# Per-event step tables and twelve collecting parts of three tiles in a four-layer graph kernel

## The reference

```python
x = _layernorm(x + attention(x, adj))            # 4 heads of 16: leaky scores, masked softmax over neighbours, relu
x = _layernorm(x + (adj + I) @ x / rowsum(adj + I))
x = _layernorm(x + adj @ (x @ W) + bias)
x = _layernorm(x + where(adj @ x > 0.5, 1, 0))
```

## Time and profile before

| what | us |
|---|---|
| median of 3 runs | 1550.73 |
| lowest, highest | 1539.59, 1557.88 |
| profiled execution, own time | 1557.14 |
| its span, first to last instruction | 1555.3 |

### The profile page before, as it was taken

The page is one execution under the profiler, slowest core; times in us unless marked ns, Lnnn a source line. Parts: engine busy times, 40 slices in busy tenths (PEclk is TensorE's granted clock), DMA queues, the critical chain, the costliest instruction groups (busy, mean ns, idle before and its releaser), DMA issues.

```text
span 1555.3 us, 20985 instructions
## 1 busy us (share of the span) xinstructions
PE 1374.7 (88%) x7296; PEld 692.2 (45%) x7296; DVE 1243.9 (80%) x1498; ACT 1223.9 (79%) x1404; POOL 1053.2 (68%) x562
## 2 busy tenths in 40 slices
PE   4798898998989999998999989899999989799766
PEld 2343444554444444444444544444444444345323
DVE  2779899778888778778897888888788888977764
ACT  1599898887878878788888878888788888878641
POOL 3177777767778766787677786777667876866412
PEclk9889899899999999999999999999999999989968
DMA  6734453243433433333343344335333433100000
GB/s 96 113 34 78 42 98 43 54 47 53 74 44 71 44 68 57 58 57 38 85 57 63 39 57 80 44 67 48 64 54 65 57 37 84 38 15 15 26 10 11
DMA packets 140879, 84.95 MB, mean 55 GB/s; under 512 B 100372, under 2 KB 130522, under 8 KB 140762
## 3 DMA queue, kind: packets, MB, share of 16 engines
q1 hardware_dynamic: 125542, 64.67, 19.9%
q0 software_dynamic: 14160, 18.51, 15.1%
q10 hardware_dynamic: 1072, 0.43, 0.1%
HBM read 103.33 MB, written 21.38 MB: 80 GB/s over the span
## 4 chain that ended last, share of the span: by engine, by line
PE 50%; POOL 12%; ACT 12%; issue 12%; DVE 11%; DMA 2%; SPq 1%; ACTq 0%; POOLq 0%; DVEq 0%
PE M L603 10%; PE Z L569 10%; PE M L658 9%; PE Z L576 8%; POOL LS L502 8%; ACT LS L750 6%; PE Z L587 4%; ACT LS L758 4%; PE Z L672 3%; PE Z L612 3%; DVE LS L912 3%; DVE RP L898 2%; POOL RSTD L507 2%; DMA adj_cast<-in_adj_dram 1%; PE Z L726 1%
## 5 line engine op out<-in xcount | busy, mean ns | idle before, releaser
L502 POOL TENSOR_TENSOR LS<-LS,MB 125x1000 f32<-125x1000 f32 x372 | 867.1, 2349 | 354.3 <-DVE LS L912 290.4
L750 ACT ACTIVATE LS<-Z 126x1000 f32<-126x1000 f32 x576 | 575.5, 1000 | 168.5 <-PE Z L576 167.3
L898 DVE TENSOR_TENSOR RP<-LS,RP 125x1000 f32<-125x1000 f32 x480 | 575.5, 1199 | 86.0 <-ACT LS L750 65.0
L758 ACT ACTIVATE LS<-LS 125x1000 f32<-125x1000 f32 x576 | 596.4, 1036 | 45.8 <-POOL LS L502 26.8
L569 PE MATMUL Z<-AT,BI 126*126 126x500 fp8e4 x1152 | 381.2, 414 | 78.0 <-ACT LS L750 50.4
L576 PE MATMUL Z<-FS,FO 128*125 128x500 f16 x1152 | 361.5, 396 | 0.0
L603 PE MATMUL M<-LS,V 126*18 126x500 f32 x2304 | 323.9, 637 | 3.9 <-ACT LS L758 3.8
L569 PEld LDWEIGHTS Z<-AT,BI 126*126 126x126 bf16 x1152 | 128.8, 143 | 391.3 <-ACT LS L750 183.0
L912 DVE TENSOR_TENSOR LS<-LS,MB 125x1000 f32<-125x1000 f32 x204 | 286.3, 1408 | 5.0
L576 PEld LDWEIGHTS Z<-FS,FO 128*125 128x125 f16 x1152 | 167.7, 146 | 99.1 <-issue 20.4
L658 PE MATMUL M<-AT,XP 125*128 125x500 fp8e4 x756 | 195.3, 381 | 0.0
(11 more groups left out here) (134 smaller groups left out, 817.7 us busy)
## 6 DMA issues: line engine op xcount, KB each, us to landing
MB<-row_maxima SPq DMA_DIRECT2D x48, 500.0 KB, 4.0
adj_cast<-in_adj_dram POOLq DMA_DIRECT2D x96, 183.1 KB, 4.5
FO<-PARTS SPq DMA_DIRECT2D x120, 46.9 KB, 2.2
FS<-PARTS SPq DMA_DIRECT2D x120, 46.9 KB, 2.1
XF<-in_x_dram SPq DMA_DIRECT2D x8, 336.0 KB
XA<-in_x_dram SPq DMA_DIRECT2D x8, 336.0 KB
out_dram<-X SPq DMA_DIRECT2D x7, 375.0 KB
AT<-adj_cast SPq DMA_TRANSPOSE x144, 2.8
```

Of the source, the lines that this page charges most:

```text
L502: nc.gpsimd.tensor_tensor(rows, rows, MB[:P, u % 2, :, :], ALU.subtract).then_inc(sub_pool, 1)
L750: nc.scalar.activation(LS[:PD, q % RL, :, :], banks("Z", q)[:PD], ACT.Prelu, alpha=SLOPE).then_inc(bent, 1)
L758: nc.scalar.activation(rows, rows, ACT.Exp, scale=0.25).then_inc(exps, 1)
L898: nc.vector.tensor_tensor(run, rows, run, ALU.max).then_inc(maxed, 1)
```

## The change

Each event gets its own step (or list of steps, one for each unit, layer or slice), in tables at the head of the file, instead of fixed distances from one start. `unit_at`, `layer_at`, `rows_at` and `feature_at` look the step up in a table handed to them. Beside this the values change, the order of the events inside a step changes on every engine, a slice is collected in 4 parts of 3 tiles (12 steps for each layer), and the add of one to the counts goes into `keep`.

```diff
-LAG = 18
-SUB_AT = LAG + 0
-EXP_AT = LAG + 2
-WEIGH_AT = LAG + 4
-RT_AT = STEPS + MAX_AT + 1
-TAKE_AT = STEPS - 1 + WEIGH_AT + 0
-G_AT = TAKE_AT + 2
-KEEP_AT = G_AT + 0
-END = QN - STEPS + KEEP_AT + 1
-CUTS = 3
+CUTS = 4
+POOL_AT, SUB_AT, EXP_AT, WEIGH_AT = 19, 19, 21, 23
+LAG = POOL_AT
+TURNED = (15, 15, 15, 15, 15, 15)
+MAXIMA = (15, 15, 15, 15, 15, 15)
+SPREAD = (16, 16, 16, 16, 16, 16)
+TAKE = (35, 35, 35, 35, 35, 35)
+SUMS = (36, 36, 36, 36, 36, 36)
+KEEP = (36, 36, 36, 36, 36, 36)
+END = QN - STEPS + KEEP[UPG - 1] + 1
-MEANS = (25, 42, 61, 79)
-CENTRE, SQUARE, SUM, POWER, SCALE, HIGH, LOW, Y0, W0 = 1, 2, 2, 3, 4, 5, 5, 9, 12
+MEANS = (24, 44, 64, 85)
+CENTRE = (25, 45, 65, 86)
+SQUARE = (26, 46, 66, 87)
+SUM = (26, 46, 66, 87)
+POWER = (27, 47, 67, 88)
+SCALE = (28, 48, 68, 89)
+HIGH = (29, 49, 69)
+LOW = (30, 50, 70)
+COLLECT = ((33, 34, 35, 36, 37, 38, 39, 40, 41, 42, 43, 44),
+           (53, 54, 55, 56, 57, 58, 59, 60, 61, 62, 63, 64),
+           (73, 74, 75, 76, 77, 78, 79, 80, 81, 82, 83, 84))
+COPY = ((36, 40, 44), (56, 60, 64), (76, 80, 84))
+BACK = ((37, 41, 45), (57, 61, 65), (77, 81, 85))
+ADD = ((37, 41, 45), (57, 61, 65), (77, 81, 85))
-FEATURES = {16: ("XT", 0), 17: ("FT", 0), 20: ("FE", 0), 21: ("XT", 1), 23: ("FT", 1), 25: ("FE", 1), 27: ("XT", 2), 28: ("FT", 2), 32: ("FE", 2)}
+FEATURES = (14, 16, 19, 20, 21, 24, 27, 30, 32)
-TRANSPOSES = {3: 1, 15: 2, 47: 3}
+TRANSPOSES = (2, 15, 43)
-for s_, steps_ in ((1, (53, 55, 57, 59)), (2, (62, 64, 66, 68)), (3, (27, 29, 31, 33))):
+LOADS = (53, 50, 57, 56, 64, 61, 66, 68, 32, 36, 39, 38)
+LOAD_SLICES = (1, 2, 3)
-LAST_ROWS = QN + 18
+LAST_ROWS = END - 6
+XF_AT, STORE_AT, XA_AT = 8, 20, 28
...
@@ SP @@
-                if turned_at(q - 1) is not None:
-                    spread_maxima(turned_at(q - 1))
+                u = turned_at(q, SPREAD, LAST_RT + 1)
+                if u is not None:
+                    spread_maxima(u)
                 if slice_at(q):
                     turn_slice(slice_at(q))
...
@@ PE, order in a step @@
-    masks, scores; make_features; collect; turn_back; turn_run; turn_sums; weigh
+    fill_z; turn_sums; make_features; collect; turn_run; turn_back; weigh
@@ ACT @@
-    square; bend; high; take; take_collect; take_features; expo
+    square; high; bend; take; take_features; take_collect; expo
@@ POOL @@
-    load; power; low; subtract
+    power; subtract; low; load
@@ DVE @@
-    maximum; keep; row_maxima; low; centre; scale; add_up; mean; add_squares; subtract; neighbours
+    scale; maximum; add_squares; centre; row_maxima; keep; low; subtract; add_up; neighbours; mean
...
@@ keep, neighbours (DVE) @@
                 if p == 0:
-                    nc.vector.tensor_reduce(DEG[:, s * ST:(s + 1) * ST], sums[:, :, :, D + 1], AX.X, ALU.add)
+                    nc.vector.tensor_scalar(DEG[:, s * ST:(s + 1) * ST], sums[:, :, 0, D + 1], 1.0, None, ALU.add)
...
-            def neighbours(b, n):
-                if n == 0:
-                    dve.wait_ge(kept_seq, 5 * (UPG * b + NS))
-                    nc.vector.tensor_scalar(DEG[:, :], DEG[:, :], 1.0, None, ALU.add).then_inc(den_seq, 1)
-                    return
-                dve.wait_ge(den_seq, 2 * b + n)
+            def neighbours(b):
+                dve.wait_ge(kept_seq, KEEPS * (UPG * b + NS))
                 nc.vector.reciprocal(RDEN[:, :], DEG[:, :]).then_inc(den_seq, 1)
```

More of the change, by code:

```diff
@@ L218, in adj_resnorm, with unit_at, turned_at @@
         block = ctx.enter_context(nc.Block())
[L220 to L227, removed]
         def graph_at(q):
             return divmod(q, SPG)
+        def unit_at(q, steps):
+            for u in range(max(q // STEPS - 4, 0), min(q // STEPS + 1, NU)):
+                if STEPS * u + steps[u % UPG] == q:
+                    return u
+            return None
+        def turned_at(q, steps, last):
+            if q >= last:
+                return NU - 1 if q == last else None
+            u = unit_at(q, steps)
+            return u if u != NU - 1 else None
         def load_at(q):
@@ L255, in layer_at, with rows_at, feature_at @@
             return None
[L257 to L262, removed]
-            return None
[L265 to L272, removed]
+        def rows_at(q, steps):
+            for l in range(NS):
+                for n, at in enumerate(steps[l]):
+                    b, off = divmod(q - at, SPG)
+                    if off == 0 and 1 <= b < B:
+                        return b - 1, l, n
+            return None
+        def feature_at(q, steps, kinds):
             b, r = graph_at(q)
-            if r in FEATURES and b + 1 < B:
-                kind, c = FEATURES[r]
+            if r in steps and b + 1 < B:
+                kind, c = kinds[steps.index(r)]
                 return kind, b + 1, c
@@ L282, in adj_resnorm @@
         for q in range(END):
[L283 to L295, removed]
+            if q < QN:
+                ring.append(("Z", q))
+            if rows_at(q, BACK):
+                ring.append(("W", *rows_at(q, BACK)))
+            if turned_at(q, TURNED, LAST_RT) is not None:
+                ring.append(("RT", turned_at(q, TURNED, LAST_RT)))
+            if unit_at(q, SUMS) is not None:
+                ring.append(("G", unit_at(q, SUMS)))
+            if feature_at(q, FEATURES, KINDS):
+                m1.append(feature_at(q, FEATURES, KINDS))
+            if rows_at(q, COLLECT) and rows_at(q, COLLECT)[2] % CUTS == 0:
+                b_, l_, n_ = rows_at(q, COLLECT)
+                m1.append(("Y", b_, l_, n_ // CUTS))
             if layer_at(q, SCALE):
@@ L411, in _ @@
                     load_features(b, 3)
[L412 removed]
+                if r == XF_AT and b + 1 < B:
                     if b:
@@ L838, in _ @@
                     square(*layer_at(q, SQUARE))
-                if q < QN and q % GROUP == 0:
-                    for n in range(GROUP):
-                        bend(q + n)
-                at = layer_at(q, HIGH)
-                if at and at[1] < 3:
-                    high(*at)
-                if unit_at(q, TAKE_AT) is not None:
-                    take(unit_at(q, TAKE_AT))
-                if y_at(q) and y_at(q)[3] == CUTS - 1:
-                    take_collect(*y_at(q)[:3])
-                if feature_at(q):
-                    take_features(*feature_at(q))
+                if layer_at(q, HIGH):
+                    high(*layer_at(q, HIGH))
+                if q < QN:
+                    bend(q)
+                if unit_at(q, TAKE) is not None:
+                    take(unit_at(q, TAKE))
+                if feature_at(q, TAKEN, KINDS):
+                    take_features(*feature_at(q, TAKEN, KINDS))
+                if rows_at(q, COPY):
+                    take_collect(*rows_at(q, COPY))
                 if 0 <= q - EXP_AT < QN:
@@ L1117, in _ @@
                     subtract(e)
-                if r in NEIGHBOURS and 1 <= b < B:
-                    neighbours(b - 1, NEIGHBOURS[r])
+                if rows_at(q, ADD):
+                    add_up(*rows_at(q, ADD))
+                if r == NEIGHBOURS and 1 <= b < B:
+                    neighbours(b - 1)
+                at = layer_at(q, MEANS)
+                if at and at[1] in CENTRED:
+                    mean(*at)
                 if q == LAST_ROWS:
-                    for n in range(2):
-                        neighbours(B - 1, n)
+                    neighbours(B - 1)
                     for c in range(NS - 1):
```

122 lines of the change are left out of this document (62 added, 60 removed).

## The result

The changed kernel takes 1571.9 us (median of 4 runs, 1567.8 to 1575.2) beside 1550.2 for the kernel before on the same chip: ratio 1.0135, interval 1.0102 to 1.0169. It is slower by 1.35%, 21 us. The forecast was 1527, faster. The profiled execution took 1573.4, its span is 1571.3 at a mean granted clock of 0.921; before it was 0.931 over 1555.3.

A forecast was written before the change was run, and what follows sets the result against it. No engine was full; ACT (plain steps) and PE (four-tile steps), coupled by two PSUM slots, set the pace. -25 - 21 - 7 + 21 + 6 + 2 = -24: 1533 us profiled, 1527 on the median; range 1484 to 1566.

The forecast's parts named there:

- SP's event: Steps 2 to 4, graphs 2 to 7: SP issues transposes ahead of the maxima; +3.5 us each, six times, +21.
- the first rival: SP's wait decides: each event in graphs 2 to 7 costs 11.9 us, not 3.5; 1579 us; chance 0.17.
- The gains: Savings from collecting in three-tile parts (-25), the third collecting layer's chain (-21) and the features (-7): 53 us.
- Third collecting layer: Its chain, where the fill of step 69 stood 3.12 us behind ACT's bend: -3 us a graph, -21.
- Parts of three: Collecting steps: 27 at 2.25 us become 36 at 2.04; 3.6 us a graph in seven graphs, -25.
- Features: Around step 28: FT follows XT at more distance, but the first layer's square stays late; -1 us a graph, -7.
- The fourth layer's chain: Moves from steps 79 to 83 to steps 85 to 89, that is 13 to 17: 0, bounds 10 either way.
- Graph 0: Step 15: 7.77 us of transposes ahead of the maxima put the first exponential at 82.3; +6 us.
- Counts' add: The add of one leaves DVE, 1.26 us for twelve columns, hidden by DVE's free time: 0.
- the longer pipeline: Pipeline one step deeper, `END` one later: +2 us with the tail.
- The second: Rival: spreading the parts gives nothing, as ACT's copies and DVE's adds share steps; 1552 us; chance 0.23.
- The third: Rival: SP's reversal is hidden wholly, as POOL and DVE catch up and PE runs ahead; 1500 us; chance 0.20.

The follow-up runs named there:

- run 5: Changed kernel with only the first transposes of a graph moved from step 2 to step 4: 1526.7 us, ratio 0.9856 to the kernel before.
- run 9: Kernel of run 8 with every layer started one step earlier (24, 44, 64, 85): 1544.3 us, ratio 0.9960 to the kernel before.
- run 8: Kernel before with parts of three tiles, layers 20 apart, rows one step later and the store at step 20: 1600.5 us, ratio 1.0336.
- run 3: Kernel of run 1 with slices collected in three parts of four tiles again, copies and adds shortened to match: 1580.3 us, ratio 1.0196.
- Run 1: Changed kernel with transposes at steps 4 and 16 instead of 2 and 15, so the maxima go first: 1530.5 us, ratio 0.9861.
- run 2: Kernel before with its transposes at steps 2 and 14 instead of 3 and 15: 1569.7 us, ratio 1.0113.
- run 11: Changed kernel with three of step 2's six transposes left ahead of the maxima and three moved behind them, to step 4: 1537.9 us, ratio 0.9928.

## Why the prediction was wrong

The forecast was 45 us too low (1572 - 1527), in two halves.

**SP's event: forecast 3.5 each and 21 in all, measured 7.2 each and 43 in all (run 5).** The mechanism was right: where, how often, and through whom. The lateness of the maxima was forecast at 8.2 (its terms, 0.9, 0.64, 0.1 and 7.7, add up to 9.3 and not 9.5, which makes 8.0); the six events show 8.0 to 9.0. The term failed in the step "ACT is held 4.1 us, and PE, two fills ahead, hides about 0.6 of it: +3.5".
- ACT is held 5.2 to 6.5 us ahead of the first exponential, 5.8 in the mean, not 4.1. The slack of 4.1 is that of before. In the new tables it is 3.1: in run 5 the exponential starts 5.4 us behind POOL's start, and POOL's subtraction takes 2.3. It was also read from a graph in which POOL begins alone; in the event POOL and DVE begin their subtractions together, when MB lands, and ACT's exponential starts at 952.10, 3.34 us after POOL's start at 948.76, not after half of 4.58. SP's two issues also stood further apart: 944.81 - 942.14 = 2.7 us from write to broadcast (1.9 to 2.7 in the six), not 1.7.
- PE stands still for 4.7 us in the event's steps, 4.1 by the whole spans, where 3.5 was forecast. It hides 5.8 - 4.7 = 1.1 of ACT's wait, not 0.6, so the two errors cancel in part.
- The missing 3.3 to 3.5 is PE's clock after the stop. The prediction knew the rows for it (1.87 against 1.03 in the earlier trace rows) and put it into the upper bound only. The sums at 1.89 and the tiles at 1.45 after the two stops of graph 5, and PE's busy time beside run 5, show that it belongs into the likeliest value: 4.1 + 3.3 = 7.4 by the two spans, 7.2 by the runs.

At 7.2 an event is just below the 7.5 at which, by the prediction, the first rival eats all gains; it did more than that only because the gains were smaller too. This is the first rival's mechanism at 0.6 of its price (7.2 of 11.9). The Trainium skill's rule in "DMA: Bandwidth & Descriptors", section "Anatomy of one DMA — SWDGE (gpsimd) path", that a semaphore wait is held on the issuing sequencer, went with that rival. The trace agrees in kind: SP's queue waits for PE's part six times, 162.0 us in all, and the maxima's write comes only behind the six issues. What makes the maxima late is those issues, 8.4 of 8.8 us in graph 5, and not the length of the wait.

**The gains: forecast 53 less 8 of small costs, 45; measured 22** (run 5: 0.0144 x 1550; 19 to 26 by its interval), so the other half of the error is here.
- *Third collecting layer, -21*: as forecast, as far as its four steps show. -3.7 a graph from steps 66 to 69, 26 us over seven graphs. In the profiles the whole gain of run 5 lies in steps 33 to 69: 90.4 us a graph in the mean of graphs 2 to 6, 95.4 before; the other steps take 0.7 more.
- *Parts of three, -25*: the price of a bare step was right, 2.04 us, and not what a run gains by it. In the old tables parts of three by themselves gave -6 (run 9) or +52 (run 8), by where a layer's rows fall; in the new ones, four tiles instead of three cost 50 (run 3). The step that failed is the working by steps: it took a part's price to be independent of what else stands in its step. In graphs 2 to 6 of run 5 the 36 collecting steps take 2.47 us in the mean, where the sum had 2.04; before, 27 took 2.69, where it had 2.25, and steps without collecting 2.43, where it had 1.81. With these means the same sum gives 0 us a graph if the nine steps between are taken at 1.81, and 5.6 if at 2.43, so it settles nothing. Between the runs the layers' places move with the parts, so how much of the new tables' gain is the parts' alone stays open.
- *Features, -7*: not there, and not for the reason given. The wait of FT for XT is gone. The square of the first layer does not stay late: ACT waits 0.0 to 1.3 us for it in graphs 2 to 6 of run 5, 2.8 before. Yet steps 24 to 28 take 15.4 us in the mean of these graphs, 14.4 before; over steps 18 to 32 it is 36.8 and 36.7. In graph 5 of run 5 the time goes to a stop that the sum did not have: PE waits 1.18 us for ACT's copy of the sums, and from 961.00 to 968.00 it works at a granted clock of 0.51, while the square, on ACT, waits for nothing:

```profile
960.20 1.20 PE L620 MATMUL Z<-E,O 128*125 128x36 f32 x8 [1.18 <-ACT O L771]
```

```profile
968.80 0.83 ACT L811 ACTIVATE XP<-Y 125x768 f32<-125x768 f32 x1
```

- *The fourth layer's chain, 0*: right as far as the steps show. Steps 13 to 17, into which it moves, take 13.1 us in run 5 and 11.2 before; steps 7 to 11, which it leaves, 11.4 and 13.5.
- *Graph 0, +6*: the time of the first exponential, 82.2 for 82.3, came out by luck. The term had the transposes hold the maxima for 7.8 us; they held them for 0.9. What came 8.9 us later were the maxima themselves, mainly by PE's wait of 6.14 us for the rows of XT, which the sum did not have. Run 1, where the maxima go first, has its first exponential at 82.3 too. The forecast's mechanism shows in run 2, in the old tables, where the exponential starts at 81.8. A price of the graph is not shown: it takes 156.2 us in after, 153.3 in run 5 and 152.5 before.
- *Counts' add, 0*, and *the longer pipeline, +2*: from the end of the last graph's 72 steps to the end, run 5 takes 103.0 us, 99.8 before, +3 in single profiles; the add has no row that would show it as late or early.

The terms above for run 5 come from single profiles, and their steps overlap, so they do not add up to the 22 us; the runs settle the total, not every part of it.

**The rivals.** The second (spreading the parts gives nothing) is borne out in part by run 9 and by collecting steps that take 2.47 us and not 2.04 in the mean; run 3 speaks against it. The third (hidden wholly) fell with run 5: without the event the kernel takes 1527, not 1500.

## What to carry to other kernels

A queue that only issues transfers is an engine with an order: before moving a transfer ahead of another, look at what it waits for, and how many issues then stand between that wait's end and the transfer that somebody needs; the whole price here was one number in a table, and setting it to 4 made the change 1.4% faster instead of 1.35% slower. Lateness isn't paid in proportion: the first microseconds fit into the slack, and the rest is paid more than once, since TensorE works on at a lower clock after it has stood, so a stall's likeliest price must hold that too. Where work is moved between steps of a tightly coupled pipeline, list what each step holds afterwards on every engine and in every ring: one step's shift was worth 58 us, ten times what the spreading itself gave. And a forecast row that comes true to 0.1 us can still have come by another way: look at when its input was ready.

## What had not been expected of the hardware

- The clock adds three quarters to the bill. In the event's steps PE is busy for 3.5 us more beside 4.7 us more of standing still; over whole spans it is 19.7 beside 24.5 us (after against run 5) and 33.7 beside 26.9 (run 3 against run 1), with the same 7296 PE instructions. Around the event the fill's half goes from 0.64 to 1.06 us behind stops of 1.75 and 2.18.
- Six transposes occupy SP's queue for 7.7 to 10.4 us (7.68 in the earlier trace rows, 8.39 in after, 9.76 and at most 10.35 in run 2) though nothing waits between them; the number to put into a sum is a range, not the shortest one.
- The same subtraction on POOL takes 3.3 us where DVE's begins some 0.05 us ahead of it (all six events of after, three of run 11), and 2.3 where POOL begins first (the other three of run 11); two of them take 4.58 in the earlier trace rows.
